# Graph-network kernel on one core: gathering rows in place, and sorting by source inside the gate stage

## What is computed

```python
x = LN(x + L0)   # (1+eps) x + segment_sum(relu(x[src] + edge_attr_48), dst)
x = LN(x + L1)   # relu(h @ W.T + b), h = ci/cj-weighted sum of x[src] over dst, or x where no edge ends
x = LN(x + L2)   # relu(agg @ W.T + b), agg = sum over src of norm * x[dst]
x = LN(x + L3)   # normalized (x + sum over src of gate * x[dst] * cutoff * node_vec[dst] / total)
# ci = rsqrt(max(out_degree, 1)), out_degree = how often a node is a source
# gate = silu(edge_attr_40 @ W1.T + b1) @ W2.T + b2 + emb[type[src]] . (emb[type[dst]] @ A.T)
```

## Time and profile before

| | us |
|---|---|
| median of three runs | 3301.34 |
| lowest, highest | 3261.16, 3327.77 |
| the profiled execution | 3252.52 |
| its span (first to last instruction) | 3250.7 |
| DVE busy, POOL busy | 2025.6, 1850.8 |
| PE busy, ACT busy | 780.1, 623.3 |

### The profile page before, as it was taken

How to read it: one execution, slowest core, us unless ns; L and a number is a source line. 1 busy time by engine, 2 the same in 40 slices (tenths; PEclk the granted TensorE clock), 3 DMA queues, 4 the chain that set the end, 5 groups by cost and what they waited for, 6 DMA issues and landing times.

```text
span 3250.7 us, 13926 instructions
## 1 busy us (share of the span) xinstructions
PE 780.1 (24%) x3478; PEld 555.3 (17%) x3478; DVE 2025.6 (62%) x2596; ACT 623.3 (19%) x1021; POOL 1850.8 (57%) x1768
## 2 busy tenths in 40 slices
PE   1182000000256563776763300000340000000000
PEld 0020000000245563444442300000240000000000
DVE  3177399877746564444553480699648969957751
ACT  0000102221223232222321100222112222221110
POOL 5703636772254547545507783777647676663776
PEclk7586555555555555555555555555555555555555
DMA  3106816762033232101100099344222212210000
GB/s 111 21 2 232 293 28 225 255 220 86 22 104 104 96 111 88 25 22 23 25 9 17 16 74 89 123 138 138 73 72 69 84 58 72 72 55 6 16 16 15
DMA packets 154357, 268.53 MB, mean 83 GB/s; under 512 B 87656, under 2 KB 112314, under 8 KB 154146
## 3 DMA queue, kind: packets, MB, share of 16 engines
q1 hardware_dynamic: 92786, 198.90, 20.8%
q0 software_dynamic: 56448, 44.04, 6.8%
q10 hardware_dynamic: 5040, 24.69, 2.1%
HBM read 135.62 MB, written 137.21 MB: 84 GB/s over the span
## 4 chain that ended last, share of the span: by engine, by line
DVE 30%; POOL 19%; issue 18%; PE 14%; another core or an unknown queue 11%; ACT 5%; DMA 2%; SPq 0%; ACTq 0%; DVEq 0%; POOLq 0%
POOL ring L429 9%; POOL out L467 6%; POOL x_table L467 4%; DVE du L1271 2%; DVE var L1277 2%; PE psT L849 2%; DVE psS L1268 2%; PE psA L902 2%; DVE sumb L1210 2%; PE psA L955 2%; DVE do L1288 1%; PE psO L864 1%; DVE var L1470 1%; DVE du L1485 1%
## 5 line engine op out<-in xcount | busy, mean ns | idle before, releaser
L467 POOL DMA_INDIRECT y_table<-sumb,put x196 | 207.6, 1059 | 293.1 <-ACT sumb L599 235.6
L429 POOL DMA_INDIRECT ring<-in_xaux,srcI x196 | 187.1, 955 | 207.7 <-ACTq L566 115.8
L467 POOL DMA_INDIRECT x_table<-sumb,put x196 | 213.4, 1089 | 154.9 <-ACT sumb L599 91.4
L429 POOL DMA_INDIRECT ring<-xa_table,dstI x196 | 222.8, 1137 | 136.0 <-ACTq L566 65.9
L429 POOL DMA_INDIRECT ring<-y_table,srcI x196 | 199.0, 1015 | 158.4 <-ACTq L549 97.1
L429 POOL DMA_INDIRECT ring<-h_by_src,zd x196 | 214.2, 1093 | 105.3 <-issue 60.0
L429 POOL DMA_INDIRECT ring<-x_table,srcI x196 | 201.8, 1030 | 115.9 <-issue 58.0
L429 POOL DMA_INDIRECT ring<-edge_records,dstI x196 | 203.1, 1036 | 112.8 <-issue 59.7
L467 POOL DMA_INDIRECT out<-sumb,put x196 | 201.5, 1028 | 107.1 <-issue 60.8
L835 PE MATMUL psG<-ident,tail 128*49 128x128 f32 x10 | 4.5, 447 | 1074.2 <-DVEq L1016 1031.5
L1277 DVE TENSOR_REDUCE var<-sq 128x28 f32<-128x1344 f32 x119 | 181.1, 1552 | 129.9 <-ACT sq L572 128.3
(11 more groups left out here) (300 smaller groups left out, 3174.4 us busy)
## 6 DMA issues: line engine op xcount, KB each, us to landing
din<-in_xaux SPq DMA_DIRECT2D x56, 728.0 KB
x_table<-do SPq DMA_DIRECT2D x56, 672.0 KB
din<-x_table SPq DMA_DIRECT2D x56, 672.0 KB
xa_table<-din SPq DMA_DIRECT2D x28, 728.0 KB
y_table<-GX SPq DMA_DIRECT2D x28, 672.0 KB
out<-do SPq DMA_DIRECT2D x28, 672.0 KB
records_by_src<-ring ACTq DMA_DIRECT2D x14, 693.0 KB
GX<-records_by_src ACTq DMA_DIRECT2D x14, 693.0 KB
```

Of the source, the lines that this page charges most:

```text
L429: pool.indirect_dma_start(ring[:, h, t, 0:w], None, table, bass.IndirectOffsetOnAxis(ap=of[:, c * H + t:c * H + t + 1], axis=0), **skip).t ...
L467: pool.indirect_dma_start(table, bass.IndirectOffsetOnAxis(ap=put[:, c * H + t:c * H + t + 1], axis=0), stage[:, h, t, :], None, bounds_ch ...
```

## The change

- The gathers of `in_xaux` and `xa_table` write straight into a table `XD` [128, 196, 52] (`gather_in_place`), each chunk with its own semaphore (`rows0` to `rows13`); ACT's copies out of the ring (`source_rows`, and five copies per chunk in L0) are gone. POOL stops after `AHEAD = 4` chunks until DVE has ended the histogram (`placed`), then goes on without a stop.
- DVE turns the degrees into weights right behind the histogram (before `deg_done`); Y1 becomes `x_with_degree`, rows of 49 numbers (`YW`), 48 features and the weight, and the 49th column goes through the product (`w1c`, K = 98). The multiplications L1312 and L1326 are gone; one store buffer `do1` serves both tables.
- `to_stage1` is called in the steps 0, 3 and 6 of the new rows and in the pairs 1, 2, 4 and 5 of the dense pass, instead of in every second pair.
- The sort leaves its place before L0. It is a generator of 165 parts now, of which the gate's half steps take up to six each (`QUOTA`, `sort_on`); PE does its 14 turns at half steps counted beforehand (`sort_groups`).
- The gate has 25 steps of eight edge columns. The types of the sources are transposed once, stored (`ZT`), and loaded broadcast over 120 partitions (`zb`); one comparison with a column of numbers makes the one-hot of 1024 edges. The products with the destination's one-hot are eight `scalar_tensor_tensor` with a sum output. The gate network works on two halves at once (`wm1` [80, 96], `wm2` [97, 96], block-diagonal). The messages are a multiplication by the gathered weight and a scan, both on DVE, in the steps 0, 1, 3, 5, 7, 8, 10, 12, 14, 16, 17, 19, 21, 23.

```diff
+            def gather_in_place(table, w, of, free=None):
+                for c in range(CE // H):
+                    if free:
+                        pool.wait_ge(free.sem, free.up())
+                    elif c == AHEAD:
+                        pool.wait_ge(S["placed"], 1)
+                    for t in range(c * H, c * H + H):
+                        pool.indirect_dma_start(
+                            XD[:, t, 0:w], None, table, bass.IndirectOffsetOnAxis(ap=of[:, t:t + 1], axis=0)
+                                ).then_inc(rows[c].sem, rows[c].add())
...
-            gather(A["xaux"], XW, srcI)
+            gather_in_place(A["xaux"], XW, srcI)
             pool.wait_ge(S["xa_done"], 1)
-            gather(XA, XW, dstI)
+            gather_in_place(XA, XW, dstI, xs_free)
...
+            dve.sem_inc(S["placed"], 1)
             one(V.tensor_scalar(none, deg[:, :], 0.0, SKIP, ALU.is_equal, ALU.mult))
...
+            ask_act()
+            one(V.reciprocal(deg, deg))
+            one(V.tensor_tensor(deg, deg, none, ALU.mult))
             dve.sem_inc(S["deg_done"], 1)
...
-            sort(own, ask_pe)
-            dve.sem_inc(S["srt_ready"], 1)
...
+            STAGED = {0: 0, 3: 1, 6: 2}
             for i in range(NBLK):
                 norm([(0, su[:, :, :])])
+                if i in STAGED:
+                    to_stage1(STAGED[i])
+            STAGED_LATER = {1: 3, 2: 4, 4: 5, 5: 6}
...
+            def sort_on(g):
+                if g + 1 in turns:
+                    return
+                for _ in range(QUOTA):
+                    if next(ordering, "end") in ("turn", "end"):
+                        break
+            def factors(k):
+                sort_on(2 * k)
+                if k + 1 < GROUPS:
+                    one_hots(k + 1)
+                if k in MESSAGES:
+                    messages(MESSAGES[k] % 2)
+                n = min(8, CE - 8 * k)
+                dve.wait_ge(mo.sem, mo.up())
+                for c in range(n):
+                    bank = ((psB, psC), (psO[0], psS))[k % 2][c // 4]
+                    V.scalar_tensor_tensor(masked[:, c, :], iotaz[:, :], zd[:, 8 * k + c:8 * k + c + 1],
+                                           bank[:, c % 4 * Z:(c % 4 + 1) * Z], ALU.is_equal, ALU.mult,
+                                           accum_out=lg[:, c:c + 1]).then_inc(own.sem, own.add())
                 dve.wait_ge(own.sem, own.now())
+                sort_on(2 * k + 1)
```

More of the change, by code:

```diff
@@ L20 @@
 XW = 52
+YW = D + 1
 RW = 99
@@ L68, in sort_turns, with sort_parts, sort_groups @@
     return turns, now
+def sort_parts():
+    parts, n = [], 9
+    for m in range(1, 16):
+        n += 2 if 2 <= m <= 8 else 1
+        if m > 8:
+            parts += [n, 1 + m - 8]
+            n = 1
+        n += min(m, 8)
+    return parts + [n]
+def sort_groups():
+    groups, g = [], 0
+    for n in sort_parts()[:-1]:
+        g += -(-n // QUOTA) + 1
+        groups.append(g)
+    return groups
 @contextmanager
@@ L228, in bass_gnn @@
         t0P = psS[:, 304:304 + CE]
+        ROWS = tuple(f"rows{c}" for c in range(CE // H))
         S = {n: sem(n) for n in (
@@ L459, in gather_x2, with scatter @@
                 gather(X2, D, of, first=2)
-            def scatter(table):
+            def scatter(table, rows_of=stage):
                 for c in range(CE // H):
@@ L652, in _ @@
+            STAGED = {0: 0, 3: 1, 6: 2}
             for i in range(NBLK):
                 norm([(0, su[:, :, :])])
-            def short1(i, last=False):
-                to_stage(M, i)
-                for q in range(PER // 2):
-                    ahead = not (last and q == PER // 2 - 1)
-                    evacuate()
-                    if ahead:
-                        evacuate((0, 1))
-                    squares(pair)
-                    if ahead:
-                        evacuate((2, 3))
-                    roots(pair)
@@ L666, in _, with short1 @@
-            evacuate()
-            for i in range(NBLK - 1):
-                short1(i)
-            short1(NBLK - 1, True)
+                if i in STAGED:
+                    to_stage1(STAGED[i])
+            STAGED_LATER = {1: 3, 2: 4, 4: 5, 5: 6}
+            def short1(n):
+                if n in STAGED_LATER:
+                    to_stage1(STAGED_LATER[n])
+                ahead = n < DBLK // 2 - 1
+                evacuate(tall=97)
+                if ahead:
+                    evacuate((0, 1), 97)
+                squares(pair)
+                if ahead:
+                    evacuate((2, 3), 97)
+                roots(pair)
@@ L671, in _ @@
+            evacuate(tall=97)
+            for n in range(DBLK // 2):
+                short1(n)
             function(t1[:, :], ACT.Sin)
@@ new lines, in factors @@
+                sort_turn(2 * k + 1)
+                pe.wait_ge(ma.sem, ma.up())
+                for j in range(4):
+                    last = T.matmul((psG, psT[1])[k % 2][:, j * 2 * D:(j + 1) * 2 * D],
+                                    h1T[:, k % 2, j * P:(j + 1) * P], wm2[:, :], start=True, stop=True)
+                last.then_inc(S["mlp_g"], 1)
+                if k + 1 < GROUPS:
+                    hidden(k + 1)
+            hidden(0)
+            for k in range(GROUPS):
+                factors(k)
@@ L1045, in _, with sort @@
             dve.sem_inc(S["flag"], 1)
-            def sort(own, turn):
+            def sort(own, ask, answered, pos):
                 def one(instruction):
@@ L1234, in _ @@
                 st[h].n = 16 * DBLK // 2
-                dve.wait_ge(st[h].sem, st[h].now())
-            one(V.tensor_scalar(deg[:, :], deg[:, :], 1.0, None, ALU.max))
-            ask_act()
-            one(V.reciprocal(deg[:, :], deg[:, :]))
             def counts(of):
@@ L1394, in _ @@
+            for k in range(GROUPS):
+                factors(k)
+            for _ in ordering:
+                pass
+            dve.sem_inc(S["srt_ready"], 1)
             dve.wait_ge(returned.sem, returned.up(2 * NBLK))
```

491 lines of the change are left out of this document (257 added, 234 removed).

## The result

The changed kernel takes 3141.54 us (median of four, 3130.97 to 3151.35); the kernel before, run beside it, 3281.25. The ratio on record, which counts fast runs alone, is 0.9702, 95% interval 0.9648 to 0.9757: faster by 3.0%. On the clock of the profiled execution (span 3149.4) the kernel lost 101.3 us, not 187.

The account below looks back on a forecast made before the run. No engine was taken to fill the span; each stage has its own limit, with POOL's long gather streams delaying everyone's semaphores. Dense pass start 1152, gate 330 and rest 1581.8 gave 3064, executed 3066, median 3115; range 2990 to 3235.

Parts of the forecast that it names:

- Histogram and front: Histogram ends at 200 instead of 260 (bounds 190 and 215), degrees ready at 217, XA's gathers end at 680.
- Start of the dense pass of L1: The dense pass of L1 starts at 779 against 867.6, a gain of 89 us.
- T + 99: Start of L1's dense pass, 99 us after T, the end of XA's gathers, forecast at 680.
- ACT's longest wait for POOL in the new rows: In the new rows ACT waits for a stage buffer until POOL scatters; about 50 to 65 us.
- the term of -51 us: Dense pass of L1: fewer stagings at 20.5 us each bring it to 373 us, bounds 345 and 410.
- Gate: Gate takes 330 us instead of 374, -44, bounds 235 and 450; free of the delay 235.
- the interpolation between two paces of the sort: Gate: between 40% pace at 19.7 us per chunk and 79% at 28, a chunk each 25 us, giving 330.
- Rival C: Slower than before: each semaphore wait in the gate costs 1.3 us more, gate 609, total 3393; chance 0.06.
- A: Rival: the gate hardly slows, gate 250 and L1 355, total 3017; chance 0.2.
- Rest: Everything after the gate: 1584.6 us less 2.8 for two degree operations, 1581.8.
- The step from the span to the median: Execution of 3066 raised by 1.5%, as the earlier runs' median 3301.34 exceeded the profiled run, to 3115.
- The rule on the shared port: Waits as a VectorE/GpSimd lock: bf16 one-hots free once POOL stops, gate near 235 us; the prediction said the trace disagrees.

Follow-up runs that it names:

- c4: Changed kernel without POOL's last twelve chunks of gathers from `x_with_degree` in the gate; 2847.82 us, ratio 0.987, on a chip without the delay.
- c1: Changed kernel with staging as before, in every second pair of the dense pass, stop kept; same kernel as a1, run again: 2795.04 us, ratio 0.9685, without the delay.
- c3: Changed kernel without the histogram stop, with a small fill that POOL waits for behind each `in_xaux` gather; 2853.01 us, ratio 0.9884, without the delay.
- b1: The changed kernel itself, run again on a chip with the delay; 3131.77 us, ratio 0.9655.
- b2: The kernel before, with only POOL's stop after four chunks of `in_xaux` until the histogram is placed; 3294.38 us, ratio 1.017.
- a4: Changed kernel without the stop for the histogram (AHEAD 14 instead of 4); 2835.86 us, ratio 0.9788, without the delay.
- a1: Changed kernel with the staging as before, seven stagings in every second pair of the dense pass; 2806.68 us, ratio 0.9676, without the delay.
- a2: Changed kernel with POOL pausing after every seventh transfer in the scatter to `x_with_degree` and its first two gathered chunks; 2921.96 us, ratio 1.0081, without the delay.
- c2: The kernel of a2 run a second time; 2904.19 us, ratio 1.0069, again without the delay.
- b3: Changed kernel with two things undone, no histogram stop and staging as before; 3164.21 us, ratio 0.9755, with the delay.

## Why the prediction was right, and where it was not

**Histogram and front: right.** 190 to 215 was given with 200 in it; it ended at 194.0, `deg` was ready at 210.7 (forecast 217), XA's first gather came at 391.2 and its last ended at 668.8 (forecast 680).

**Start of the dense pass of L1: right in kind, 23 us too late.** T + 99 was forecast, the pass began at T + 87 with T 11 us earlier: -112 instead of -89. One sign missed: ACT's longest wait for POOL in the new rows was 18.3 us in after and 38.9 without the delay (c4), where 50 to 65 was given. And the prediction counted this wait as one that comes with the change, and did not ask what it buys. The runs price it: without the delay the pass begins 81 us behind T with the new places of the staging (c4: 614.7, 695.8) and 20 us behind it with the old ones (c1). POOL's scatter ends earlier in return, at 994.6 instead of 1254.8, and that helps nobody: POOL then stands 189 us before the ring, until the gate gives it back.

**Dense pass of L1, the term of -51 us: wrong.** It was +35 (459.2 for 373). The step that failed is "a staging costs (412 - 14 x 19.2) / 7 = 20.5 us, of which the waits for a stage are 207.3 / 14 = 15 each". The 207.3 us of the earlier trace rows are those of the whole span; 8.1 of them lie in this pass. So the 20.5 was no price of a staging but, for the most part, the delay that 28 scatters cause, and it does not go away with three of seven stagings: the scatters stay. The sum has a slip besides: 269 + 102.5 + 12 at the end is 384, not 373. Two things make up the 459:

- The pass without delay and with the old staging is 311 us (c1), so the seven stagings cost (311 - 12 - 14 x 19.2) / 7 = 4.3 us each. The new places make it 346 (c3, c4), 35 us more. ACT's waits for a stage in the pass are 52.1 us in c4 and 14.8 in c1, 37 us apart: ACT asks for a stage before POOL has caught up.
- The delay adds 459 - 346 = 113 us, for 137 scatters and 28 gathers beside the pass, 0.69 us each. In b1 it is 413 - 346 = 67 (0.41 each). The kernel before was not profiled without the delay; with c1's 311 in its place, an estimate, the delay was 424 - 311 = 113 for 196 scatters and 27 gathers (0.51 each), and in b2 60 for 213 (0.28). So by this estimate a pass pays some 0.3 to 0.7 us for each DMA that POOL issues beside it. The prediction's own upper bound, 410, was too low by the same fault.

With these prices the pass would have been 311 + 35 + 0.51 x 165 = 430, and the span 3121.

**Gate: right.** 330 was forecast, 324.1 measured (b1: 312.0). "Free of the delay the gate would take 235": 240.9 (a4) and 242.6 (c3), though DVE's own work in it was 207.4 us and not 232. DVE was busy 64% of it (just under the 65 forecast), PE 46% (under 60). What the delay held up was other than forecast, though. DVE is idle for 117 us of the gate, and for 35 in c3 without the delay. Of the 81 us between them the 120 compare steps of the sort account for 22 (26.5 here, 4.2 in c3), and DVE's waits for PE's type products (L1464) for 40 (43.2 here, 2.8 in c3). ACT's silu (L714), whose input is PE's product, waits 183.4 us with nobody named (8 times, up to 30.9) and 228.6 in all, against 122.4 in c3 (groups of like instructions, 1214.9 to 1539, then the chain of waits):

```profile
L1113 DVE TENSOR_TENSOR do<-do 128x128 f32<-128x128 f32 x120 | 35.3, 294 | 26.5 <-remote 11.0 <-DVE do L1114 7.1 <-issue 4.0
L1464 DVE SCALAR_TENSOR_TENSOR sq<-iotaz,zd,psB 128x120 f32<-128x120 bf16 x48 | 13.3, 335 | 39.0 <-remote 33.1 <-issue 5.6 <-DVE du L1433 0.2
```

```profile
ACT do L714 <- remote: 183.4, 8, 30.9
```

So the interpolation between two paces of the sort gave the right sum, with some luck, for a stage that is held up mostly at its hand-overs between engines. Rival C, a toll of 1.3 us on each wait, falls with it: the compare steps pay some 0.2 us each; so does A on the chip of the result, while on a chip without the delay A describes the gate.

**Rest: 1610.4 for 1581.8, and not by the change.** The difference lies before the first gather of the records, where POOL waits for the stores of `edge_records`. First the kernel before (beside the result), then after, then the kernel before with the stop (b2):

```profile
2021.46 0.98 POOL L429 DMA_INDIRECT ring<-edge_records,dstI  x1 [40.87 <-DMA edge_records<-MG]
```

```profile
1921.33 0.99 POOL L475 DMA_INDIRECT ring<-edge_records,dstI  x1 [63.43 <-DMA edge_records<-MG]
```

```profile
2035.03 0.99 POOL L429 DMA_INDIRECT ring<-edge_records,dstI  x1 [54.50 <-DMA edge_records<-MG]
```

40.9 to 63.4 us, with either program (c1 43.7 and a1 56.5 are one and the same kernel). On one chip the rest was 1601.4 (b2) and 1604.3 (b1), the program before and the one after.

**The step from the span to the median** added 1.5%, 49 us, since the profiled execution of before was below its median. That of after was the longest of its four. This error went the other way than the L1 term and hid most of it: 3115 is 27 us off the median, while for the profiled execution 3066 was forecast and 3151.4 measured, 85 more. That the median came so near is luck.

**The rule on the shared port.** The trace of after has ACT standing 43.05 us after PE's transposes beside POOL's stream, and on two chips the bf16 one-hots run at 0.5 us a turn beside POOL's gathers. The Trainium skill, page "SBUF — State Buffer", section "SBUF: two separate sides", has VectorE in a two-port mode and GpSimd excluding each other for a whole instruction, and nobody else held up. Both observations speak against its being the cause here.

**What stays open.** Why the delay was there on two occasions and not on two others; each was on one chip, so that the chip and the occasion can't be told apart. And whether pauses (a2, c2) or slower gathers (c3) would prevent it, since both were run only where it was absent. That it is POOL's stream that delays the others in the dense pass and the gate rests on their records (long waits while POOL issues, short ones behind it) and on the difference between the chips; only in the histogram did changing POOL's gathers (b2, b3) test it. That the old staging is better is shown without the delay: c1 and a1 have ratios of 0.9685 and 0.9676, where after comes to about 0.993 (c4's span with c3's gate, 2846.8 + 242.6 - 227.0 = 2862, some 2864 us, on 2885.34; an estimate, as after itself was not run there). With the delay it is shown only with the stop undone: b3's 67 us from XA to the gate, of which the gate gives 9 back. After with the old staging and the stop should come to about 58 us less than b1 there; this was not run. Where it ran it is the fastest kernel of its group both times.

## What to carry to other kernels

A row of waits belongs to a stage only if it was asked for that stage: 207.3 us of waits in the whole span were 8.1 in the pass they were used for, and that was the term that failed. Starting a transfer early is worth nothing if its end has slack (189 us here) and an engine that others need must wait to feed it: leave such a wait where it is short. A gain that comes from avoiding a disturbance lasts only where there is the disturbance: this change is worth 3.0 to 3.5% where POOL's streams delay the others, and an estimated 0.7% where they do not.

## What was not expected of the hardware

The same kernel took 3235 and 3281 us on two occasions and 2885 and 2898 on two others, and within one occasion its runs lay 1.3 to 2.2% apart on the first kind and 0.2% on the second. The records of the changed kernel, with POOL gathering, show the difference first in the histogram: a turn of the histogram takes 5.6 us on the one kind (5.01 of them waiting), 0.5 on the other. The wait reaches PE, ACT and DVE alike; it appears some 17 us after a stream begins (29.7 and 46.7 in after), outlasts it by 6 to 15 us (1031.4 to 1037.1 in after, 164.6 to 179 in before), and inside long streams a single hand-over from PE to ACT took up to 43 us. Beside the dense pass of L0, where the gathers come one in 1.42 us, a small delay is there. Two pairs of after, then two of c1 (timeline of DVE):

```profile
445.01 3.15 DVE L1348 SCALAR_TENSOR_TENSOR GX<-du,c2e,srs 128x1344 f32<-128x1344 f32 x2 [1.55 <-remote]
...
461.83 3.15 DVE L1348 SCALAR_TENSOR_TENSOR GX<-du,c2e,srs 128x1344 f32<-128x1344 f32 x2 [1.52 <-DVE srs L1338]
```

```profile
455.85 3.15 DVE L1348 SCALAR_TENSOR_TENSOR GX<-du,c2e,srs 128x1344 f32<-128x1344 f32 x2
...
469.75 3.15 DVE L1348 SCALAR_TENSOR_TENSOR GX<-du,c2e,srs 128x1344 f32<-128x1344 f32 x2
```

16.8 us a pair with the delay, 13.9 without (14.5 was forecast): in a pair of after DVE stands some 1.5, 0.9 and 1.0 us before L1348, L1326 and L1329, in one of c1 only about 0.5 before L1326. It costs the end nothing, since the new rows wait for POOL anyway.
